# Redrawn order of five instruction queues in a two-layer graph attention kernel

## The reference

```
# layer 0, one head                      # layer 1, eight heads of 64
h  = x @ W                               q, k, v = x1 @ W{q,k,v}.T + b{q,k,v}
e  = leaky_relu(h@a0 + (h@a1).T, 0.2)    s  = q @ k.T / 8, masked by adj
al = softmax(e masked by adj)            p  = softmax(s)
x1 = layernorm(x + concat(al @ h, h))    y  = layernorm(x1 + (p @ v) @ Wo.T + bo)
```

## Time and profile before

| | |
|---|---|
| median of 3 runs | 3111.64 us (3110.63 to 3115.23) |
| profiled execution | 3113.64 us, span of its trace 3111.8 us |
| TensorE busy | 2959.5 us, 95% of the span |
| VectorE busy | 2748.2 us, 88% |
| ScalarE busy | 2426.8 us, 78% |
| GpSimd busy | 2070.7 us, 67% |
| DMA queue, share of 16 engines | 63.2% |

### The profile page before, as it was taken

The page is one execution under the profiler, slowest core; times in us unless marked ns, Lnnn a source line. Parts: engine busy times, 40 slices in busy tenths (PEclk is TensorE's granted clock), DMA queues, the critical chain, the costliest instruction groups (busy, mean ns, idle before and its releaser), DMA issues.

```text
span 3111.8 us, 58284 instructions
## 1 busy us (share of the span) xinstructions
PE 2959.5 (95%) x19084; PEld 2499.3 (80%) x19084; DVE 2748.2 (88%) x6556; ACT 2426.8 (78%) x5031; POOL 2070.7 (67%) x1415
## 2 busy tenths in 40 slices
PE   5999999999999999999999999999999999999995
PEld 4788888888888888888888888888888888888874
DVE  5898998988999998998989999889999989989884
ACT  4877888777887777887777877778887778877774
POOL 2567676667776667766667766677766667766664
PEclk8999999999999999999999999999999999999997
DMA  3666666666666666766666766566766666665654
GB/s 129 210 213 232 227 240 217 219 216 233 226 239 222 208 227 225 243 230 216 213 224 221 248 223 221 211 228 232 244 222 217 220 224 223 244 225 211 221 208 159
DMA packets 306413, 685.39 MB, mean 220 GB/s; under 512 B 56896, under 2 KB 90432, under 8 KB 273344
## 3 DMA queue, kind: packets, MB, share of 16 engines
q1 hardware_dynamic: 306112, 681.68, 63.2%
HBM read 375.40 MB, written 306.18 MB: 219 GB/s over the span
## 4 chain that ended last, share of the span: by engine, by line
PE 57%; DVE 20%; DMA 8%; issue 6%; ACT 4%; POOL 4%; SPq 1%; ACTq 0%; POOLq 0%; DVEq 0%
PE R_bank L646 32%; PE O_bank L735 10%; PE S_bank L716 8%; DVE blocked L1033 4%; PE L_bank L646 4%; DMA turned_lo_prob<-scratch 3%; DVE alpha L958 3%; PE L_bank L637 3%; DVE qk_pair L930 3%; DVE prob L1013 2%; DMA scratch<-blocked 2%; DVE scale_cols L919 2%; POOL o_half L1087 2%; DVE o_half L1041 2%; DVE stats L913 1%
## 5 line engine op out<-in xcount | busy, mean ns | idle before, releaser
L1093 POOL TENSOR_TENSOR turned_lo_prob<-turned_lo_prob,turned_hi_prob 128x1024 fp32r<-128x1024 f32 x512 | 1251.9, 2462 | 551.8 <-ACT turned_hi_prob L764 549.4
L852 ACT ACTIVATE prob<-prob,small_cols 128x512 f32<-128x512 f32 x1024 | 729.4, 714 | 172.6 <-DVE r_cols L1022 157.2
L1033 DVE STREAM_TRANSPOSE blocked<-prob 128x512 f32<-128x512 f32 x1024 | 696.5, 694 | 61.1 <-ACT prob L852 39.7
L1013 DVE CUSTOM_DVE_ANT_0 prob<-S_bank,mask 128x512 f32<-128x512 f32 x1024 | 675.5, 683 | 15.0 <-PE S_bank L716 10.1
L764 ACT ACTIVATE turned_hi_prob<-turned_lo_prob 128x1024 fp32r<-128x1024 f32 x512 | 534.9, 1052 | 50.5 <-DMA turned_lo_prob<-scratch 40.1
L735 PE MATMUL O_bank<-turned_hi_prob,v_st 128*128 128x256 f32 x2048 | 519.5, 291 | 44.1 <-DVE o_half L1041 23.3
L735 PE MATMUL O_bank<-turned_lo_prob,v_st 128*128 128x256 f32 x2048 | 505.5, 284 | 0.0
L735 PEld LDWEIGHTS O_bank<-turned_hi_prob,v_st 128*128 128x128 f32 x2048 | 393.0, 192 | 92.1 <-POOL turned_lo_prob L1093 66.3
L716 PE MATMUL S_bank<-qk_pair 64*128 64x512 f32 x3072 | 435.5, 411 | 12.9 <-DVE qk_pair L930 8.7
L646 PE MATMUL R_bank<-wv,x1T 128*128 128x256 f32 x3072 | 419.4, 287 | 15.6 <-DVE v_st L909 15.6
L646 PEld LDWEIGHTS R_bank<-wv,x1T 128*128 128x128 f32 x3072 | 383.1, 189 | 34.7 <-DVE v_st L909 22.5
(11 more groups left out here) (90 smaller groups left out, 4494.5 us busy)
## 6 DMA issues: line engine op xcount, KB each, us to landing
scratch<-blocked SPq DMA_DIRECT2D x256, 1024.0 KB, 4.4
turned_lo_prob<-scratch SPq DMA_DIRECT2D x256, 1024.0 KB, 5.6
tokens<-xT SPq DMA_DIRECT2D x128, 256.0 KB, 5.8
tokens<-x SPq DMA_DIRECT2D x128, 256.0 KB, 3.1
r_wide<-r_scratch SPq DMA_DIRECT2D x512, 64.0 KB, 3.2
out<-tokens SPq DMA_DIRECT2D x128, 256.0 KB, 4.3
r_scratch<-r_cols SPq DMA_DIRECT2D x256, 16.0 KB
tokens<-adj SPq DMA_DIRECT2D x1, 1024.0 KB, 6.4
```

The costliest lines, as they stand in the source:

```text
L852: act.activation(prob_tile(R, s), prob_tile(R, s), ACT.Exp, bias=negmax[:, slot:slot + 1], scale=-1.0, accum_out=psum_row[:, ph % 2, j:j + ...
L1013: dve.tensor_tensor_reduce(prob_tile(R, s), score_bank(R, s)[:, :], mask[:, s % 8 // 2, :], -SCALE, HUGE, ALU.add, ALU.min, negmax[:, slot ...
L1033: dve.transpose(blocked[:, ph % 2, :, :, 2 * (s % 2) + s % 4 // 2, :].rearrange("p d c i -> p c d i"), prob_tile(R, s).rearrange("p (d c i ...
L1093: pool.tensor_tensor(lo_ap, lo_ap.bitcast(F32), turned_hi_prob[:, 2 * a:2 * a + 2, :, :].bitcast(F32), ALU.subtract).then_inc(p_lo, 1)
```

## The change

Only the tables of names change. Every piece is issued as often as before, with the same instructions and the same semaphores; where it stands in its queue is new, on all five engines, in the round, the prologue, the last round and the ending. A few lines of the diff, of the tables of PE and ACT in a round, on which the prediction rests; the rest is of the same kind:

```
 TENSOR_PLAN = (
-    "N k1 weigh weigh C0 scores scores O0",
...
-    "E3 weigh weigh scores B0 q4 k4 weigh",
...
+    "k1 N weigh weigh scores scores O0 O1",
...
+    "weigh E3 weigh scores B0 q4 k4 weigh",
...
 SCALAR_PLAN = (
-    "N pre0 exp evQ1 aexp0 exp lows pre1",
...
-    "hi evW0 pre3 hi evW1 turn C2 aexp3",
...
+    "evQ1 exp exp lows N pre0 turn exp",
+    "exp exp hi hi aexp0 pre1 exp C0",
...
+    "evQ2 aexp2 C1 exp turn fin0 pre3 exp",
+    "hi hi evW0 C2 aexp3 evW1 lows fin1",
```

More of the change, by code:

```diff
@@ L53 @@
 TENSOR_PLAN = (
[4 rows of a table removed]
-    "weigh scores scores D3 q3 k3 weigh weigh",
[5 rows of a table added]
     "E0 scores scores E1 V0 scores E2 V1",
[2 rows of a table removed]
[2 rows of a table added]
     "scores weigh weigh B3 q1",
@@ L64 @@
 SCALAR_PLAN = (
[3 rows of a table removed]
-    "exp C1 exp fin0 turn lows exp aexp2",
[6 rows of a table removed]
[L75 to L78, removed]
+    "evQ1 exp exp lows N pre0 turn exp",
[9 rows of a table added]
+    "B0 exp exp exp A1 evQ4 turn exp",
+    "lows A2 B1 hi exp turn hi B2",
+    "A3 evV2 evV3 exp exp exp lows hi",
+    "B3 hi exp turn exp",
 )
 VECTOR_PLAN = (
[10 rows of a table removed]
[L91 to L96, removed]
[10 rows of a table added]
+    "reduce reduce E1 reduce vt sum reduce E2",
[4 rows of a table added]
+    "vt sum inv reduce B3 reduce",
 )
@@ L99 @@
     "norm turn lo lo lo lo norm yrs",
[5 rows of a table removed]
[5 rows of a table added]
 )
 SP_PLAN = (
[6 rows of a table removed]
[6 rows of a table added]
 )
 LAST_TENSOR_PLAN = (
[L115 to L119, removed]
+    "k1 weigh weigh scores scores O0 O1 scores",
+    "scores weigh weigh O2 O3 q2 k2 weigh",
+    "weigh scores scores W0 W1 W2 scores weigh",
+    "weigh scores W3 q3 k3 weigh weigh scores",
+    "scores scores weigh scores weigh weigh weigh weigh",
     "weigh",
@@ L122 @@
 LAST_SCALAR_PLAN = (
[L123 to L131, removed]
+    "exp evQ1 exp lows turn hi hi exp",
+    "exp exp exp exp lows exp hi hi",
+    "evQ2 exp exp turn hi hi evW0 exp",
+    "lows evW1 exp evW2 exp exp turn exp",
+    "lows hi hi evW3 exp fin0 evQ3 exp",
+    "exp fin1 turn hi hi lows fin2 exp",
+    "exp exp exp exp turn fin3 hi hi",
+    "exp exp lows exp turn hi hi lows",
+    "turn lows hi hi turn",
 )
 LAST_VECTOR_PLAN = (
[L134 to L137, removed]
[4 rows of a table removed]
-    "reduce vt reduce vt vt sum reduce inv",
-    "vt vt reduce reduce reduce vt inv sum",
-    "vt vt sum inv sum",
+    "reduce vt reduce evQ1 sum vt inv reduce",
[5 rows of a table added]
+    "reduce vt vt vt reduce reduce reduce inv",
+    "sum evW3 evQ3 vt vt vt reduce reduce",
+    "reduce sum vt inv vt reduce vt reduce",
+    "vt vt reduce reduce reduce sum inv vt",
+    "vt vt inv sum sum",
 )
 LAST_GPSIMD_PLAN = (
[1 row of a table removed]
[2 rows of a table added]
     "turn lo lo norm turn lo lo norm",
[2 rows of a table removed]
[1 row of a table added]
     "turn",
@@ L179 @@
 SCALAR_PROLOGUE = (
[5 rows of a table removed]
-    "B3 exp exp",
[5 rows of a table added]
+    "exp exp B3",
 )
 VECTOR_PROLOGUE = (
[6 rows of a table removed]
[6 rows of a table added]
 )
 GPSIMD_PROLOGUE = (
-    "A0 lrs bo0 bo1 bo2 bo3 A1 A2",
-    "A3",
+    "lrs A0 A1 bo0 A2 bo1 bo2 A3",
+    "bo3",
 )
 SP_PROLOGUE = (
-    "ld0 ld1 ld2 ld3 rs sv",
+    "ld0 ld1 ld2 ld3 sv rs",
 )
@@ L209 @@
 VECTOR_ENDING = (
-    "sum evO0 evO1 yst0 yst1 evO2 yst2 evO3",
-    "yst3 yrs",
+    "sum evO0 evO1 yst0 evO2 yst1 yst2 evO3",
+    "yst3 yrs0",
 )
 GPSIMD_ENDING = (
-    "norm turn yrs",
+    "norm turn yrs0",
 )
```

## The result

| | before | after |
|---|---|---|
| time, median of 4 runs each (us) | 3111.96 | 3027.88 |
| lowest to highest run | 3110.63 to 3115.23 | 3024.24 to 3028.9 |
| profiled execution, and its span | 3113.64, 3111.8 | 3028.9, 3027.1 |

The new order is faster: the ratio of the times is 0.9724, 95% [0.9712, 0.9735], some 84 us. I had forecast 3065 with a range of 3030 to 3118: the right direction, a gain of 84 instead of 47, and a time just under the low end.

A forecast was written before the change was run, and what follows sets the result against it. TensorE was taken as the bound, with 91.65 us of work in a 93.70 round. Gains of 2.67 less losses of 1.10 net 1.57 a round, 47 us over 30 rounds: forecast 3065, range 3030 to 3118.

The forecast's parts named there:

- (a): At `O0` TensorE loses 0.94 us a round waiting for `turn` on GpSimd; 0.85 taken as won.
- (b): At `W3` TensorE loses 0.61 us a round waiting for `evW1` on VectorE; all taken as won.
- (c): At `weigh` behind `k3` TensorE loses 0.70 us a round waiting for `sum`; all taken as won.
- (d): At `scores` behind `E0` TensorE loses 0.51 us a round waiting for `evQ3`; all taken as won.
- Sum of the losses: New waits of TensorE in the new order, three terms, 1.10 us a round, subtracted from gains of 2.67.
- `weigh` 8 and `B0`: Tail of the first layer, tight on two counts: new waits of 0.25 us a round for both together.
- `C2`, `D2`, `D3`: Pieces newly put ahead of evacuations there: new waits of 0.15 us each, 0.45 a round.
- the unnamed 0.40: New waits elsewhere that the trace of before cannot show: 0.40 us a round, bounds 0 and 2.76.
- The ends of the run: The start and the last 114 us, redrawn too: change of 0, with 8 us to either side.
- R1: Rival, chance 0.2: `lrs` (L919) keeps meeting `lo` on GpSimd; net 0.32 us a round, 3102 us.
- R2: Rival, chance 0.13: unnamed new waits come to 1.8 us a round; net 0.17 a round, 3107 us.
- R3: Rival, chance 0.12: the probabilities' store and load take 12.06 us, costing 3.75 a round; slower, 3177 us.

The follow-up runs named there:

- the single replacements: Old order with only the minimum replaced by a transpose and a reciprocal, 3058.22 us; old order with only L919 and L921 replaced by reciprocals, 3088.95 us.
- the kernel without the lock: New order with the two-input minimum replaced by a transpose and a reciprocal, and L919 and L921 by reciprocals: 3028.61 us, ratio 0.9718.

## Why the prediction was right in direction and wrong in size

**The bound and its four losses: right.** TensorE's full round and the four places with their causes stood as read, and the single replacements assign (a), (b) to the minimum and (c), (d) to `lrs`.

**The gains: 2.67 forecast, 2.64 measured.** By the timeline of after:
- (a) `O0` and `O1` take 1554.66 - 1548.86 = 5.80. In before the row behind them is

```profile
1601.11 0.60 PE L637 MATMUL L_bank<-ident,alpha 128*128 128x128 f32 x4
```

so they took 1601.11 - 1594.45 = 6.66: 0.86 won (0.85 forecast).
- (b) the four `W` take 1583.05 - 1577.29 = 5.76, 1.44 each. My pace of 1.51 for such a group was too long: two make 2.88, so the place had lost 3.63 - 2.88 = 0.75, and all of it is won (0.61).
- (c) gone: 2.81, 0.70 won.
- (d) 0.53 instead of 0.86: 0.33 won (0.51). Four transposes followed by scores take 1574.17 - 1573.64 = 0.53 behind `C2` too; the 0.35 that I used is what they take with a group of `wv` behind them.

**The step that failed is "Sum of the losses: 0.25 + 0.45 + 0.40 = 1.10".** Measured, the named ones come to 0.23 instead of 0.70, and the unnamed ones are not there:
- `weigh` 8 and `B0`: `V1` to `weigh` 1604.79 - 1603.16 = 1.63 against 1.51, so 0.12; the scores ahead of `B0` 1608.38 - 1607.38 = 1.00 against 0.89 for the like pair of before, so 0.11. Together 0.23, for a forecast of 0.25.
- `C2`, `D2`, `D3` (0.45 forecast): nothing that counts. The stretch ahead of each takes 1573.64 - 1571.72 = 1.92, 1585.02 - 1583.05 = 1.97 (a pair of `weigh` has 2.00 by the pace) and 1588.67 - 1587.07 = 1.60, an undisturbed pair of scores. The `yrs` (L919) that the new order puts ahead of `C1`'s evacuation, and which I had named as a reason, takes 0.16 there:

```profile
1571.88 0.16 DVE L919 TENSOR_SCALAR scale_cols<-meanvar 128x4 f32<-128x4 f32 x1
```

- the unnamed 0.40: it came out as a gain. 2.64 - 0.23 = 2.41, and the round became 2.85 shorter, so 0.44 more went than the named places hold. Part of it lies in old waits too small for my list. One is ahead of the old `E3`, in TensorE's timeline of before:

```profile
1651.14 1.68 PE L646 MATMUL R_bank<-wv,x1T 128*128 128x256 f32 x12
1652.89 0.63 PE L637 MATMUL L_bank<-ident,tokens 128*128 128x128 f32 x4
```

1.75 against 1.51, so 0.24. The rest, 0.20, I have not placed one by one. It is of the size of what the late rounds cost: the shortest rounds of before and after differ by 93.43 - 90.88 = 2.55, the means by 94.14 - 91.28 = 2.86, so some 0.3 of the gain comes from rounds that are late less often or by less. What makes them so is not separated here.

In round numbers, 1.28 us a round were missing in the forecast (2.85 against 1.57): 0.45 from `C2`, `D2` and `D3`, 0.02 from the other named pair, 0.84 from the unnamed term and its sign, less 0.03 from the gains. I had summed a chance of a near miss at every tight place as though all of them missed. That the gains came to the forecast's sum is in part luck: (b) won 0.14 more and (d) 0.18 less than I had.

**The ends of the run: right.** Hardly anything there, within the 8 us to either side.

**The rivals.** R1 is refuted by L919, and by timing: it was put behind a `reduce`, and in the round of after it comes at the very end of the pair of `lo`,

```profile
1594.44 0.17 DVE L919 TENSOR_SCALAR scale_cols<-meanvar 128x4 f32<-128x4 f32 x1
```

```profile
1589.75 4.78 POOL L1093 TENSOR_TENSOR turned_lo_prob<-turned_lo_prob,turned_hi_prob 128x1024 fp32r<-128x1024 f32 x2 [2.01 <-ACT turned_hi_prob L764]
```

the pair ending at 1589.75 + 4.78 = 1594.53. It starts 0.09 us ahead of the pair's recorded end and is not stretched. By the rows of before an earlier start would have met the pair, so R1 was near. The one two-input operation that still falls into a pair of `lo` is `red` 2. The two rows, of VectorE and of GpSimd, in after:

```profile
1563.18 1.07 DVE L958 CUSTOM_DVE_ANT_1 alpha<-alpha,mask 128x512 f32<-128x512 f32 x1
```

```profile
1563.83 5.07 POOL L1093 TENSOR_TENSOR turned_lo_prob<-turned_lo_prob,turned_hi_prob 128x1024 fp32r<-128x1024 f32 x2 [5.66 <-ACT turned_hi_prob L764]
```

5.07 instead of 4.78, and the kernel without the lock, which has no such meeting, is no faster. In R1 the Trainium skill's rule ("SBUF — State Buffer", section "Who interferes with whom") made the minima half of the cure; replacing them alone gave 57 of the 84, replacing L919 and L921 alone 27, so the runs agree that both kinds contend.

R2 (new waits that eat the gain) is refuted by the round of 91.35 with 91.31 of TensorE in it. R3 (the round trip of the probabilities) did not come as a loss: ScalarE's wait for the load, over the whole span, was before

```profile
ACT turned_hi_prob L764 <- DMA turned_lo_prob<-scratch: 40.1, 47, 2.5
```

and is after

```profile
ACT turned_hi_prob L764 <- DMA turned_lo_prob<-scratch: 27.7, 39, 4.7
```

The longest of these waits has grown, from 2.5 to 4.7. What R3 names is there in single rounds, as the chain above with its load of 6.54 shows, but at a small price: the largest wait of TensorE that is left in after between 1200 and 2200 is the one for `lo`, 1.9 in four waits. That is 0.17 a round, where R3 would have taken 3.75.

## What to carry to other kernels

Where a kernel is bound by one engine and still loses a little every round, compare each row's shortest and longest length: alike instructions whose length doubles while another engine runs may be waiting inside themselves, as here, and a list of idle times does not show it. Such a meeting can be cured by what stands next to it, either by moving the instruction clear of the other engine's or by putting ahead of it work that does not contend. When the waits of a tight schedule are priced, don't add an allowance for every near miss. And a gain that equals its forecast is not yet a test of it: one wait may have gone beside the expected one and another come.

## What the runs showed of the hardware

- A VectorE minimum with both inputs in SBUF, or the `tensor_scalar` of L919, and a GpSimd `tensor_tensor` keep each other out for a whole instruction, small ones too: an L919 of 4 columns, 0.17 us alone, was held for up to 1.85, and GpSimd's `norm` for 0.86 by a `red` that came first.
- A minimum with one input in PSUM and one in SBUF is not held. Of before, where GpSimd is busy for 67% of the span, over the whole run:

```profile
L1013 DVE CUSTOM_DVE_ANT_0 prob<-S_bank,mask x1024: 650/686/695, 76.3 to 3061.4; 128x512 f32<-128x512 f32 x171
```

- Nor is a reciprocal with one SBUF input, in the place where the `tensor_scalar` of L919 was. In the old order with the scales replaced:

```profile
L919 DVE RECIPROCAL scale_cols<-meanvar x64: 173/174/178, 53.5 to 3083.6; 128x4 f32<-128x4 f32 x64
```
